# Full-size attention: a tile's values begin half a slot later in TensorE's order

## What is computed

```python
def _attention(x):
    B, C, H, W = x.shape
    xf = x.reshape(B, C, H * W)
    scores = jnp.einsum('bcn,bcm->bnm', xf, xf)
    attn = jax.nn.softmax(scores, axis=-1)
    out = jnp.einsum('bnm,bcm->bcn', attn, xf)
    return out.reshape(B, C, H, W)
for scale in (4, 2, 1):
    block = _avg_pool(x, scale)
    block = _attention(block)
    block = jax.image.resize(block, (B, C, H, W), method='bilinear')
    out = out + block
```

## Time and profile before

| what | value |
|---|---|
| median of 3 runs | 5644.61 us (5643.97 to 5648.42) |
| the profiled execution: its own time | 5637.48 us |
| the profiled execution: span of the trace | 5635.7 us |
| first and last turn of the full-size attention (L1929) | at 4143.2 and 5632.6 us of the span |
| between them: PE, DVE, ACT, POOL busy | 1369.72, 1017.99, 1091.95, 1065.07 us of 1489.40 |
| between them: granted TensorE clock, DMA share, GB/s | 0.99, 1.10, 192 |

### The profile page before, as it was taken

One profiled execution on the slowest core, in us unless ns is written; L12 is line 12 of the kernel. 1 busy time (PEld: TensorE's weight loads), 2 busy tenths in 40 slices (PEclk: granted clock), 3 DMA queues, 4 the chain that ended last, 5 costly groups with the idle time before them and its releaser, 6 DMA issues. The chain is left out here.

```text
span 5635.7 us, 68281 instructions
## 1 busy us (share of the span) xinstructions
PE 5006.5 (89%) x22742; PEld 2621.1 (47%) x22742; DVE 4530.2 (80%) x6402; ACT 3450.4 (61%) x4188; POOL 4494.9 (80%) x2067
## 2 busy tenths in 40 slices
PE   6999999999999999999999997982779999899898
PEld 3444444444444444444444444530446666566565
DVE  8999999999999999999999997005767677677665
ACT  5666676676676676666566562000667777677676
POOL 6999999999999999999999995001557777677676
PEclk9999999999999999999999999795889999999999
DMA  5656666566566555565566562592789999999999
GB/s 206 211 211 212 210 211 213 209 211 215 208 211 214 208 212 214 208 212 213 209 212 214 209 212 97 216 407 50 165 156 191 195 194 192 193 193 190 189 192 184
DMA packets 1416309, 1137.13 MB, mean 202 GB/s; under 512 B 1212666, under 2 KB 1222546, under 8 KB 1408532
## 3 DMA queue, kind: packets, MB, share of 16 engines
q1 hardware_dynamic: 1411480, 1131.52, 72.2%
q10 hardware_dynamic: 4478, 1.25, 0.2%
HBM read 814.23 MB, written 21.09 MB: 148 GB/s over the span
## 5 line engine op out<-in xcount | busy, mean ns | idle before, releaser
L822 POOL TENSOR_TENSOR mamba_state<-mamba_state,mamba_c_row 128x1024 f32<-128x1024 f32 x1024 | 2404.9, 2366 | 107.3 <-DVE mamba_state L795 96.8
L693 PE MATMUL mamba_y_ps<-mamba_state,ident 128*128 128x512 f32 x4096 | 1954.4, 602 | 146.9 <-POOL mamba_state L822 145.6
L795 DVE TENSOR_TENSOR_SCAN mamba_state<-mamba_decay,mamba_b_ps 128x1024 f32<-128x1024 f32 x704 | 1609.9, 2287 | 96.3 <-DVE mamba_b_ps L781 1.9
L1957 POOL TENSOR_TENSOR l3s_el<-l3s_s_sb,l3s_eh 128x1024 f16<-128x1024 f32 x512 | 1083.3, 2135 | 473.3 <-ACT l3s_s_sb L1942 454.3
L693 PEld LDWEIGHTS mamba_y_ps<-mamba_state,ident 128*128 128x128 f32 x4096 | 744.2, 189 | 995.6 <-issue 659.2
L1965 DVE TENSOR_SCALAR_CACHE_REDUCE l3s_s_sb<-l3s_s_ps 128x512 f32<-128x512 f32 x1024 | 705.3, 690 | 453.2 <-PE l3s_s_ps L1898 447.8
L1912 PE MATMUL l3s_o_ps<-l3s_vt,l3s_et 128*128 128x257 f16 x4096 | 806.0, 275 | 132.0 <-DMA l3s_et<-l3s_el 90.9
L781 DVE TENSOR_TENSOR mamba_b_ps<-mamba_dtu,mamba_b_ps 128x1024 f32<-128x1024 f32 x704 | 849.4, 1207 | 0.6 <-PE mamba_b_ps L681 0.6
L1941 ACT ACTIVATE l3s_eh<-l3s_s_sb,l3s_shift 128x1024 f16<-128x1024 f32 x512 | 583.5, 1140 | 429.3 <-DVE l3s_shift L1976 405.7
L795 DVE TENSOR_TENSOR_SCAN mamba_state<-mamba_b_ps,mamba_b_row 128x1024 f32<-128x1024 f32 x320 | 729.1, 2278 | 103.4 <-POOL mamba_b_row L816 103.3
L771 ACT ACTIVATE mamba_decay<-mamba_dt,mamba_A 128x1016 f32<-128x1016 f32 x704 | 782.9, 1133 | 12.5 <-DVE mamba_state L795 9.4
(11 more groups left out here) (325 smaller groups left out, 5153.7 us busy)
## 6 DMA issues: line engine op xcount, KB each, us to landing
mamba_c_row<-mamba_c_rows SPq DMA_DIRECT2D x1024, 512.0 KB, 3.8
mamba_b_row<-mamba_c_rows SPq DMA_DIRECT2D x320, 512.0 KB, 4.8
l_ring_a<-in_L_conv_W SPq DMA_DIRECT2D x28, 1024.0 KB, 11.0
l2b_ring_b<-in_L_conv_W SPq DMA_DIRECT2D x26, 1024.0 KB, 11.1
l_ring_a<-in_L_conv_W SPq DMA_DIRECT2D x14, 704.0 KB, 12.7
l2b_ring_b<-in_L_conv_W SPq DMA_DIRECT2D x13, 704.0 KB, 12.7
l_ring_a<-in_L_conv_W SPq DMA_DIRECT2D x14, 640.0 KB, 12.1
l2b_ring_b<-in_L_conv_W SPq DMA_DIRECT2D x13, 640.0 KB, 12.1
```

Of the source, the lines that this page charges most:

```text
L693: last = nc.tensor.matmul(y_ps[:, half(h)], C["ident"][:, :], state[:, s % STATES, half(h)], start=False, stop=(s == S - 1))
L795: nc.vector.tensor_tensor_scan(state[:, s % STATES, :], by, add, 0.0, ALU.mult, ALU.add).then_inc(s_scan, 1)
L822: nc.gpsimd.tensor_tensor(state[:, s % STATES, :], state[:, s % STATES, :], c_row[:, s % C_ROWS, :], ALU.mult).then_inc(s_hc, 1)
L1957: nc.gpsimd.tensor_tensor(el[:, part, off:off + EXPW], s_sb[:, par, j * EXPW:(j + 1) * EXPW], eh[:, part, off:off + EXPW], ALU.subtract).t ...
```

## The change

The lags and places in the slots are changed; no instruction is added or taken away. On TensorE the values of a tile no longer run from step 0 to step 7 of one slot. They begin at step 4 of slot s (tile s-2, first half) and end at step 3 of the next one (there tile s-3, second half). What follows the values moves too: VectorE's inverse of tile s-3 to ahead of step 4, ScalarE's `act_low` of s-3 to after piece 3, VectorE's output of s-3 to after step 7, the turn on TensorE to after step 1 and the update of X to after step 3, both for tile s-4. One slot more stands at the end. The DMAs keep their order and their waits.

```diff
-        INVERSE_AT, OUT_AT, TURN_AT, UPDATE_AT = 0, min(1, NB - 1), min(2, NB - 1), min(4, NB - 1)
+        HALF_NB = NB // 2
+        INVERSE_AT, OUT_AT, TURN_AT, UPDATE_AT = HALF_NB, NB - 1, 1, 3
 
         def pe_slot(pe, b, i, par):
-            now, values, done = (behind(b, i, par, k) for k in (0, 2, 3))
+            now, begun, ending, done = (behind(b, i, par, k) for k in (0, 2, 3, 4))
             for kb in range(NB):
                 if now:
                     pe_scores(pe, *now, kb)
+                values, step = (begun, kb - HALF_NB) if kb >= HALF_NB else (ending, kb + HALF_NB)
                 if values:
-                    pe_values(pe, *values, kb)
+                    pe_values(pe, *values, step)
                 if done and kb == TURN_AT:
                     pe_turn(pe, *done)
...
-                if done and j == 0:
+                if done and j == EXN - 1:
                     act_low(act, *done)
...
-            now, done = (behind(b, i, par, k) for k in (0, 3))
+            now, ending, done = (behind(b, i, par, k) for k in (0, 3, 4))
             for kb in range(NB):
-                if done and kb == INVERSE_AT:
-                    dve_inverse(dve, *done)
+                if ending and kb == INVERSE_AT:
+                    dve_inverse(dve, *ending)
...
-                if done and kb == OUT_AT:
-                    dve_out(dve, *done)
+                if ending and kb == OUT_AT:
+                    dve_out(dve, *ending)
...
                 if done and kb == UPDATE_AT:
-                    if full and j == 3:
-                        wait(dve, s_band, 4 * (b * (QT // 4) + k + 1))
+                    if full and j == 0:
+                        wait(dve, s_band, 4 * (b * (QT // 4) + k))
                     dve_update(dve, *done)
...
-            for i in range(3):
+            for i in range(4):
```

## The result

The changed kernel takes 5599.23 us (median of 4 runs, 5597.72 to 5600.13), beside 5644.29 us for the kernel before: a ratio of 0.9921, 95% interval 0.9905 to 0.9936. That is 45 us or 0.8% less, where 70 us were forecast, and inside the range. The profiled execution took 5600.13 us, 37.3 less than the one of before.

The account below looks back on a forecast made before the run. Bound by latency from last scores to values: 121 steady slots x (11.50 - 10.95) = 67 us plus 3 at the images, 70 off the profiled 5637.5 gives 5567.5; expected median 5575 us, range 5530 to 5630.

Parts of the forecast that it names:

- What bounded the kernel: Last stage: latency from a tile's last scores to its values makes TensorE wait about 0.87 us of each 11.50 us slot.
- The values' place: TensorE's values start four steps, 5.3 us, later; the wait for `el` goes, worth up to 0.87 us a slot.
- The cap: SyncE's queue of transposes becomes the next limit: between 10.4 and 11.06 us a slot, taken as 10.95.
- upper row: SyncE's unbroken steady run of seven transposes: 2.64 us each, 11.06 us a slot with stores and loads.
- a sign (2.5 or more): SyncE in the new trace: its issues should have a median of 2.5 us or more.
- lower row: SyncE's unbroken run of six transposes at an image's start: 2.47 us each, 10.4 us a slot.
- Images and ends: Three image starts and the stage's end: the values' later place saves at most 1 us per image, 3 us; the end nothing.
- Rival A: TensorE becomes the bound as issues shorten to about 2.47 us; slot 10.63 plus a little, 5525 us; chance 0.13.
- Rival B: Transfers were the bound all along, around 192 GB/s; slots stay 11.4 to 11.5, time within 11 us of 5645; chance 0.11.
- Rival C: TensorE's turn waits for VectorE's output, behind `act_low` and ScalarE's fourth piece; slower, 5721 us at 1.5 us per slot; chance 0.07.
- Single buffers: Sign of being wrong: ScalarE or GpSimd waits for landings (`eh`, `el`, one buffer) by more than the 10.95 us allows.

## Why the prediction was right, and where it was off

*What bounded the kernel.* Right: a chain of latency from the last scores to the values. A step of 1.33 us of slack gives most of the gain, and SyncE's gaps went from 93 to 3 us.

*The values' place.* Right: the waits for `el` fell from 84.3 to 17.9 us (under 30 forecast).

*The cap.* The mechanism was right, and this is the term that was off. I named SyncE's queue as the next bound, with 10.4 and 11.06 us as its bounds, and took 10.95. It measures 11.16 in the first image and 11.21 over all four. Without the 0.5 us for stores and loads the first is 10.66 / 4 = 2.67 us for each transpose, just above even the upper row's 2.64. Of the 67 us for the steady slots, 121 x 0.28 = 34 came. The slot lies just outside the 10.75 to 11.15 of the forecast, and the time less than 1 us inside its 5550 to 5600: that it still fell there is partly luck. The issues of the first image in the changed kernel, beside the earlier trace rows:

```profile
L2167 SPq DMA_TRANSPOSE l3s_et<-l3s_el x59: 1731/2455/3942, 4145.7 to 4469.6; - x59
L2165 SPq DMA_TRANSPOSE l3s_et<-l3s_eh x59: 1532/2449/3692, 4148.6 to 4471.5; - x59
```

The medians that I leaned on (2.44 and 2.51) hardly moved: 2.45 and 2.46 here, 2.47 and 2.53 over the stage. So the median, which I had as a sign (2.5 or more), tells little; the mean of the issues went from 2.50 to 2.60. The lower row, 2.47, came from a stretch without a fetch, and the upper one from a single run of seven. The kernel before held a better row. Its transposes from the third issue after a gap on, 234 of them between 4150 and 5490 us with no gap above 0.2 us behind, are spaced 2.67 us: 4 x 2.67 + 0.5 = 11.2 us.

*Images and ends.* Of the 3 us at the images about 2 came, beyond the gain of the steady slots. I had written nothing for the start, where the first turn moved 5 us later, nor for the last two turns, which came 4 us closer together.

*Rival A* (TensorE as the bound, 5525 us) is what half the `el` transposes give, 5512.56 us. It needs the queue out of the way. *Rival B*, that the transfers were the bound before, is wrong: the queue went from 192 to 197 GB/s. But it was nearer than its chance said, since only 0.28 to 0.34 of the 0.87 us were to be had. *Rival C* showed itself as 16.9 us of waits of the turn and cost nothing, since the queue covers it. *Single buffers*, which the prediction gave as the sign of being wrong: ScalarE and GpSimd wait for landings now, but SyncE has no gaps, and with a light queue the same buffers allow 10.63 us.

## What to carry to other kernels

When a wait is to be removed, add up for each queue and engine what one round of the loop asks of it, and take the mean, not the median, over all stretches in which it never waits. Before you lean on one short stretch, look at what else the DMA engines did in it: the fast one here had no instruction fetch. Little slack can be enough when the next bound is near; here one step of eight gave three quarters of the gain. After such a change, waits appear on every engine ahead of the new bound. They are its back-pressure, and to remove one of them gave nothing here.

## What the runs showed of the hardware

Relieving SyncE of 0.5 us of issuing per slot let the issues of the transposes stretch and gave 0.12 us, while taking the transfers away, 5% of the bytes, gave 0.42 us. TensorE's instruction count changes the rate of DMA transposes: with 80 of 177 matmuls gone a slot is 0.28 us shorter (11.21 to 10.93), while cutting the same matmuls to 16 columns does nothing. The fetches of instructions carry it: a transpose of 512 KB in flight together with a 16 KB fetch landed after 5.91 us in the changed kernel, the others after 4.72.
